# ACT reads the side banks behind the second exp of a burst; VectorE clips every fourth head of weights

## The reference

```python
x = L0_attn_x; xn = _layernorm(x, axis=-1)
return x + attn(xn) + ffn(xn)
# attn: scores = q k^T / sqrt(8); exp(clip(scores - max, -50, 50)) / (sum + 1e-6), times v, times Wout
# ffn:  q, k with rotary embedding; softmax attention, times Wo; x = rmsnorm(src + sa)
#       shared = swiglu(x W_shared_in) W_shared_out
#       h = swiglu(x W1_shared); routed = sum over 8 experts e of (h W2[e]) * w[:, e], two experts nonzero
#       out = rmsnorm(x + shared + routed)
```

## Time and profile before

| | before |
|---|---|
| median of 3 runs | 2111.24 us |
| the profiled execution's own time | 2110.22 us |
| its span, first to last instruction | 2108.4 us |
| TensorE busy | 1957.9 us (93%) |
| VectorE busy | 1629.0 us (77%) |
| ACT busy | 1442.8 us (68%) |
| GpSimd busy | 1135.9 us (54%) |
| granted TensorE clock, mean | 0.993 |

### The profile page before, as it was taken

One profiled execution on the slowest core, in us unless ns is written; L12 is line 12 of the kernel. 1 busy time (PEld: TensorE's weight loads), 2 busy tenths in 40 slices (PEclk: granted clock), 3 DMA queues, 4 the chain that ended last, 5 costly groups with the idle time before them and its releaser, 6 DMA issues.

```text
span 2108.4 us, 43905 instructions
## 1 busy us (share of the span) xinstructions
PE 1957.9 (93%) x10694; PEld 602.4 (29%) x10694; DVE 1629.0 (77%) x2948; ACT 1442.8 (68%) x2993; POOL 1135.9 (54%) x1695
## 2 busy tenths in 40 slices
PE   4998899999999999999999999999999999999885
PEld 1222223232332323233232323323232222323232
DVE  3878897878879787887978788797978879797421
ACT  0367677777777777777777777777777777777752
POOL 1352637456473746647374664737466473746434
PEclk9999999999999999999999999999999999999997
DMA  2101010101101010110101010010101001010000
GB/s 92 43 27 50 28 53 31 56 27 53 36 24 56 29 57 26 52 36 25 56 28 58 26 55 32 26 56 27 59 26 54 31 27 56 26 56 18 22 0 16
DMA packets 79167, 81.93 MB, mean 39 GB/s; under 512 B 14716, under 2 KB 66172, under 8 KB 78844
## 3 DMA queue, kind: packets, MB, share of 16 engines
q1 hardware_dynamic: 78984, 80.20, 11.2%
HBM read 11.36 MB, written 4.19 MB: 7 GB/s over the span
## 4 chain that ended last, share of the span: by engine, by line
PE 71%; DVE 12%; issue 7%; ACT 6%; POOL 2%; SPq 1%; DVEq 1%; ACTq 0%; DMA 0%; POOLq 0%
PE o_ps L501 19%; PE score_ps L467 19%; PE side_ps L580 10%; DVE negmax L757 7%; PE side_ps L567 6%; PE shift_ps L482 5%; PE side_ps L549 5%; PE side_ps L516 3%; ACT weights L614 3%; DVE x L785 2%; PE side_ps L553 2%; PE side_ps L538 2%; PE side_ps L572 1%; ACT spread L649 1%; DVE stats L846 1%
## 5 line engine op out<-in xcount | busy, mean ns | idle before, releaser
L757 DVE TENSOR_REDUCE negmax<-score_ps 128x1 f32<-128x512 f32 x2048 | 1308.4, 682 | 350.0 <-PE score_ps L467 326.4
L614 ACT ACTIVATE weights<-shift_ps 128x512 f32<-128x512 f32 x2048 | 1161.2, 599 | 517.9 <-PE shift_ps L482 491.1
L482 PE MATMUL shift_ps<-qt,kt 51*128 51x512 bf16 x2048 | 691.3, 387 | 46.7 <-ACT weights L614 42.3
L467 PE MATMUL score_ps<-kt,qt 48*128 48x512 bf16 x2048 | 658.1, 393 | 58.6 <-DVE negmax L757 32.3
L954 POOL TENSOR_SCALAR weights<-weights 128x2048 f32<-128x2048 f32 x256 | 485.1, 1895 | 138.5 <-ACT weights L614 109.8
L501 PE MATMUL o_ps<-weights,vt 128*32 128x512 f32 x4096 | 550.1, 610 | 0.3 <-POOL weights L954 0.3
L467 PEld LDWEIGHTS score_ps<-kt,qt 48*128 48x128 bf16 x2048 | 131.7, 94 | 683.7 <-DVE negmax L757 544.6
L580 PE MATMUL side_ps<-w_sb,hidden 128*128 128x512 f32 x512 | 252.2, 617 | 9.9 <-ACT spread L649 8.1
L482 PEld LDWEIGHTS shift_ps<-qt,kt 51*128 51x128 bf16 x2048 | 150.4, 93 | 220.7 <-ACT weights L614 210.5
L649 ACT ACTIVATE spread<-side_ps,gate 128x128 f32<-128x128 f32 x512 | 159.8, 377 | 26.3 <-PE side_ps L580 26.3
L567 PE MATMUL side_ps<-x1T,w_up_sb 128*128 128x512 f32 x256 | 148.2, 665 | 6.3 <-DVE hidden L817 4.7
(11 more groups left out here) (111 smaller groups left out, 1452.0 us busy)
## 6 DMA issues: line engine op xcount, KB each, us to landing
qt<-q_parts SPq DMA_DIRECT2D x768, 32.0 KB
kt<-k_parts SPq DMA_DIRECT2D x768, 32.0 KB
x_in<-in_x_dram SPq DMA_DIRECT2D x16, 256.0 KB, 2.7
xn_mid<-xn_new SPq DMA_DIRECT2D x16, 256.0 KB, 2.4
xn_old<-xn_mid SPq DMA_DIRECT2D x16, 256.0 KB, 2.4
res_new<-in_x_dram SPq DMA_DIRECT2D x16, 256.0 KB, 2.6
res_old<-res_new SPq DMA_DIRECT2D x16, 256.0 KB, 2.7
out_dram<-out_sb SPq DMA_DIRECT2D x16, 256.0 KB, 2.6
```

The source lines that it names most:

```text
L467: pe.matmul(score_ps[:, score_bank(a, t), :], qt[a][row:row + HROWS, slot, 128 * tile:128 * tile + 128], kt[a][row:row + HROWS, slot, :], ...
L482: pe.matmul(shift_ps[:, t % 2, :], kt[a][row:row + HROWS + MROWS, slot, 128 * tile:128 * tile + 128], qt[a][row:row + HROWS + MROWS, slot, ...
L614: act.activation(weights[:, i % 8, tile, :], shift_ps[:, t % 2, :], ACT.Exp, scale=SCALE).then_inc(weighed, 1)
L757: dve.tensor_reduce(negmax[:, i // 8, tile, i % 8:i % 8 + 1], score_ps[:, score_bank(a, t), :], AX.X, ALU.max, negate=True).then_inc(max_t ...
```

## The change

ACT's readers of side banks move by one to three steps: from the step after the job (an even step, whose exp is the first of its burst) to a later one. Most come to stand at odd steps; tanh moves from up + 1 to up + 3, and VectorE's product from up + 2 to up + 3; the expert scalings from job + 1 and + 2 to job + 2 and + 4; the high parts of q_plain and k_plain from + 1 to + 2, with VectorE's rests one step later. VectorE gets `clip` for heads 3, 7, 11 and 15, each in two halves of two tiles, with the floor alone; GpSimd keeps the other twelve, with floor and ceiling. The value groups of plain heads wait for both.

```diff
                     if a == PLAIN:
-                        pe.wait_ge(clip_pool, cnt(b, lag, H, 4 * quad + 4))
+                        pe.wait_ge(clip_pool, cnt(b, lag, 12, 3 * quad + 3))
+                        pe.wait_ge(clip_dve, cnt(b, lag, 8, 2 * quad + 2))
...
 (ACT, even half)
-                    if t == after("even", "max_rope1"):
+                    if t == after("even", "max_rope1", 2):
-                    part(b, 0, t, "q_rope", after("even", "qs_rope", 5), ROPE, roped[:, 0, :], q_parts, True)
+                    part(b, 0, t, "q_rope", after("even", "qs_rope", 4), ROPE, roped[:, 0, :], q_parts, True)
-                        if t == after("even", f"up{n}") and live(b, -2):
+                        if t == after("even", f"up{n}", 3) and live(b, -2):
-                    if t == 18:
+                    if t == 19:
-                    part(b, 0, t, "k_rope", after("even", "ks_rope", 11), ROPE, k_rest[:, :], k_parts, False)
-                    if t == after("even", "back_plain"):
+                    part(b, 0, t, "k_rope", after("even", "ks_rope", 10), ROPE, k_rest[:, :], k_parts, False)
+                    if t == after("even", "back_plain", 2):
-                    if t == after("even", "max_plain0"):
+                    if t == after("even", "max_plain0", 2):
-                    if t == 50:
+                    if t == 51:
-                        if t == after("even", f"v{n}", 1) and live(b, 0):
+                        if t == after("even", f"v{n}", 2) and live(b, 0):
...
 (ACT, odd half; max_plain1, back_rope, max_rope0 and the two copies of o_ps likewise one step on)
-                    part(b, 1, t, "q_plain", after("odd", "q_plain"), PLAIN, bank("q_plain"), q_parts, True)
-                    part(b, 1, t, "q_plain", after("odd", "q_plain", 3), PLAIN, q_rest[:, :], q_parts, False)
-                    part(b, 1, t, "k_plain", after("odd", "k_plain"), PLAIN, bank("k_plain"), k_parts, True)
+                    part(b, 1, t, "q_plain", after("odd", "q_plain", 2), PLAIN, bank("q_plain"), q_parts, True)
+                    part(b, 1, t, "q_plain", after("odd", "q_plain", 4), PLAIN, q_rest[:, :], q_parts, False)
+                    part(b, 1, t, "k_plain", after("odd", "k_plain", 2), PLAIN, bank("k_plain"), k_parts, True)
-                            if t == after("odd", f"exp{n}", 1 + half):
+                            if t == after("odd", f"exp{n}", 2 + 2 * half):
                                 weight_experts(b, n, half)
...
 (VectorE)
+            def clip(b, i, part):
+                if live(b, 0):
+                    dve.wait_ge(weighed, cnt(b, 0, 2 * UNIT, NT * i + 2 * part + 2))
+                    half = weights[:, i % 8, 2 * part:2 * part + 2]
+                    dve.tensor_scalar(half, half, FLOOR, None, ALU.max).then_inc(clip_dve, 1)
...
                     maximum(b, PLAIN, t)
+                    if t in (1, 2):
+                        clip(b + (-1), H - 1, t - 1)
...
-                        if t == after("even", f"up{n}", 2) and live(b, -2):
+                        if t == after("even", f"up{n}", 3) and live(b, -2):
...
                     maximum(b, ROPE, t)
-                    for job, rest, quarter in (("q_plain", q_rest, 9), ("k_plain", k_rest, 13)):
+                    if t > 16 and t % 16 in (1, 2):
+                        clip(b, t // 4 - 1, t % 16 - 1)
+                    for job, rest, quarter in (("q_plain", q_rest, 10), ("k_plain", k_rest, 14)):
...
 (GpSimd: the calls clip(b + (-1), 15), clip(b, 3), clip(b, 7) and clip(b, 11) are gone)
```

More of the change, by code:

```diff
@@ L273, in layer_kernel @@
         clip_pool = sem("clip_pool")
+        clip_dve = sem("clip_dve")
         valued = sem("valued")
@@ L711, in odd @@
                     weigh(b, 0, PLAIN, t)
-                    if t == after("odd", "max_plain1"):
+                    if t == after("odd", "max_plain1", 2):
                         copy_max(b, "max_plain1")
@@ L721, in odd @@
                         for half in range(2):
-                            if t == after("odd", f"exp{n}", 1 + half):
+                            if t == after("odd", f"exp{n}", 2 + 2 * half):
                                 weight_experts(b, n, half)
-                    if t == 18:
+                    if t == 19:
                         copy_o(b, "o_rope1", "o_rope0", 0)
-                    if t == after("odd", "back_rope"):
+                    if t == after("odd", "back_rope", 2):
                         copy_side(b, "back_rope", headsT[:, :])
-                    if t == after("odd", "max_rope0"):
+                    if t == after("odd", "max_rope0", 2):
                         copy_max(b, "max_rope0")
-                    if t == 50:
+                    if t == 51:
                         copy_o(b, "o_plain0", "o_rope1", 0)
@@ L1044, in even @@
             def even(b):
-                clip(b + (-1), 15)
                 if live(b, -3):
@@ L1080, in odd @@
                 third(b, 1, PLAIN, 1, k_rest, k_parts)
-                clip(b, 3)
                 clip(b, 4)
@@ L1087, in odd @@
                 mix(b, 2)
-                clip(b, 7)
                 if live(b, -1):
@@ L1101, in odd @@
                 mix(b, 5)
-                clip(b, 11)
                 mix(b, 6)
```

## The result

| | before | after |
|---|---|---|
| median | 2110.26 us (4 runs, 2108.23 to 2111.75) | 2277.01 us (4 runs, 2270.54 to 2290.05) |
| the profiled execution's own time | 2110.22 us | 2270.54 us |
| its span | 2108.4 us | 2268.8 us |
| granted TensorE clock, mean | 0.993 | 0.970 |

A forecast was written before the change was run, and what follows sets the result against it. TensorE's program order, busy 93%, was taken as the bound. Per round 10.95 us lost less 4.6 gained gave +6.3; 14 full rounds +88, ramps' clips some 2, on 2110.2: forecast 2201 us, 80% range 2150 to 2258.

The forecast's parts named there:

- six bank waits: TensorE waits at exp1, exp2, exp5 (1.6 us each), down0 (1.57), v0 (1.73) and k_plain (1.0), every round.
- part 2: Later readers release side banks later; lost per round: 4.8 us at expert jobs, 3.3 at down0 and v0, 1.0 at k_plain.
- the copies' gain: Ten places per round, late because a copy or scalings stood before a second exp, come on time: 3.5 us gained.
- the 0.95 us of the clips at steps 1 and 2: Even half's start: two VectorE half clips of 0.62 us, less 0.3 us of gaps, lose 0.95 us per round.
- the 0.9 us of VectorE's stretch: Around even steps 45 to 53, up2's later product and clips at 49/50 make VectorE late: 0.9 us lost per round.
- part 3: VectorE's clips: 8 more instructions per round at 0.70 us each; 0.95 and 0.9 us lost, 1.1 us gained per round.
- steps 17/18 ... slack enough: VectorE's clips at steps 17/18 lie ahead of exp0's 2.4 us job, so they cost nothing.
- clips fight GpSimd: Rival, 17%: VectorE's clips wait up to 1.9 us for GpSimd or cost 1.22 us; 3.0 us per round more, 2243 us.
- the gain of 1.1 us: Four scaled products at step 46, no longer beside a GpSimd clip, let bursts after steps 48 and 50 come on time.
- a round of 132 us: Sign that gains or clips were misjudged; the forecast itself had a round of 128 to 130 us.
- Late copies without a gain: Rival, 8%: ACT's backlog only moves one burst on, so the 3.5 us gain per round is missing: 2250 us.
- Stalls absorbed: Rival, 5%: VectorE and ACT catch up while TensorE stands, leaving 2.75 us gained per round: 2072 us.

The follow-up runs named there:

- experiment 3: The changed kernel, VectorE clips kept, with exp0, exp1, exp4, up0, up3 and q_plain read early again, all else late: 2099.96 us, ratio 0.9931 to before.
- kernel 2: The changed kernel with all sixteen clips on GpSimd again, moved readers kept: 2237.94 us, ratio 1.0592 to before.
- kernel 1: The kernel before with VectorE's clips of heads 3, 7, 11 and 15 alone, no copy moved: 2133.94 us, ratio 1.0094 to before.
- kernel 5: The kernel before with only the expert scalings late, at job + 2 and + 4: 2200.74 us, ratio 1.0419 to before.
- experiment 6: The changed kernel with exp0 alone released early, scaled by both pairs at job + 2: 2229.79 us, ratio 1.0547 to before.
- experiment 7: The kernel before with exp0's scalings alone late, at steps 20 and 22 instead of 19 and 20: 2144.36 us, ratio 1.0119 to before.
- experiment 8: The changed kernel with six banks released early, all clips on GpSimd, tanh of up1 to up3 at up + 2: 2084.79 us, ratio 0.9856 to before.
- kernel 9: As experiment 8, with the copies of xnT and x1T one step later: 2072.74 us, ratio 0.9801 to before.
- kernel 11: As kernel 9, with the clip of head 11 given to VectorE in halves at odd steps 49 and 50: 2044.78 us, ratio 0.9654 to before.
- kernel 10: As kernel 9, with GpSimd's clip of head 11 ahead of the mix of expert 5: 2059.6 us, ratio 0.9729 to before.

## Why the prediction was wrong in size

**Right: what decides.** That TensorE would stand at six bank waits, and how long, held to 0.1 us a piece in the burst distances (part 2); the copies' gain held (3.5 forecast, 3.7 measured, the shift's waits for ACT down from 408 to 205); so did the 0.95 us of the clips at steps 1 and 2, and the 0.9 us of VectorE's stretch. VectorE's half clip was put at 0.70 us from three rows of other operations, and undisturbed it takes 0.68. Undoing the six waits turned +8.0% into -0.7% (experiment 3), so the sign came out right for the stated reason.

**Wrong in part 3, "steps 17/18 ... slack enough".** I checked that VectorE had time there, not what GpSimd was doing. Head 3's second half meets clip 4 and takes 2.28 us: 1.41 x 14 = 20 us. The rival "clips fight GpSimd" had the mechanism and 17%, but priced it at steps 1/2, 33/34 and 49/50. Of those, 33/34 shows halves of 0.75 and 0.92 us without harm to TensorE, the others none in the loop. The sign that I had given for it, a mean over 0.9 us for the clip's row, is there, at 922 ns:

```profile
L767 DVE TENSOR_SCALAR weights<-weights 128x1024 f32<-128x1024 f32 x128 | 118.0, 922 | 0.0
```

**Wrong in part 3, the gain of 1.1 us.** "That clip is gone from GpSimd and clip 10 will be over": the clip in the earlier trace rows was clip 10. Instead of -1.1 came +0.55, 1.65 x 14 = 23 us. It could have been counted in the trace of before: the clips of a round stand in the order of the list. That it became a loss, and not nothing, depends on the phase: kernels 2 and 3 show neither here, kernel 1 +0.52, and kernel 5, without a clip on VectorE, +0.36. What sets it wasn't isolated.

**Left out: the clock.** The sum put it at nothing: no term and no rival had it, and the rows of before gave no hint, its clock being 0.993. For rounds 2 to 14, which have no edge effects, the account is: 140 us more than before; forecast 13 x 6.3 = 82; the steady terms came out at 8.9 a round (the table's 9.7 less the 0.8 that is the clock's) instead of 6.35, 13 x 2.55 = 33 more; 25 are left for 18 falls, 1.4 us each, near the 1.6 of the rounds with a fall behind exp2 and the 1.6 to 2.2 of experiments 5 to 7. Outside these rounds: -5 us in rounds 0 and 1, and +25 from round 15 on, where the forecast had 8. Of these 25, 7.5 lie in round 15, near the forecast's 6.3, and 17.9 behind the last score, where 2 were forecast and all is busy time at the lower clock (above). 140 - 5 + 25 = 160, the difference of the spans. So the clock has some 25 + 18 = 43 us of it, more than either of the two wrong terms. The sum was made against one profiled execution; the median of after lies 6.5 us over its profiled one, whose mean clock, 0.970, is the highest of the four (the others 0.960 to 0.965).

**The signs.** The prediction named a round of 132 us as the sign that gains or clips were misjudged; the round is 133.6, and it was so, with the clock beside it. TensorE's busy share is 86% where near 90 was forecast, and GpSimd is 98 us less busy where it was 120.

**The rivals.** Late copies without a gain: refuted by the ten places, 3.7 us shorter together. Stalls absorbed: refuted, each wait costs its whole length, and the six together 8.9 us a round.

## What to carry to other kernels

When a reader is moved later, ask first when its bank is written again, and let only the readers with a spare bank go late: nearly the same edit cost 5.9% or gained 1.4%, by six places out of some thirty (experiments 2 and 8). Before giving VectorE an SBUF-to-SBUF operation, list what GpSimd runs at that very microsecond, by name and index; a start 0.15 us behind GpSimd's made 2.28 us of 0.68. And where a sum adds pauses to TensorE, put a price on its clock too: in this kernel pauses of 1.5 us cost a quarter to a half more than they lasted (26.1 us for 20.5, 142 for 115, 91 for 62 in experiments 7, 3 and 5).

## What the runs showed of the hardware that I had not expected

- A single pause of TensorE of 1.5 us, in a kernel that keeps it over 90% busy, can be followed by 3.4 us at half its clock; 13 rounds had 3 such falls with one pause a round, 18 with six; kernels 1 and 3, without these pauses, had 3 and 4, behind VectorE's longer stretch at the even half's start. An extra pause of 1.76 us (kernel 9) was followed by 6.8 us and more.
- GpSimd, 55% busy over the span, bounds the end of a round once TensorE's other waits are gone; a clip taken from it, which I had put at nothing, was worth 28 us between kernels 9 and 11, 15 of them against the reordered list of kernel 10.
- A VectorE pass of 128x1024 fp32 with one SBUF source takes 0.68 us, and 2.28 (at most 2.34) beside a GpSimd clip of 1.90 that began first. It goes the other way too: in kernel 1 GpSimd's clip took 2.36 us, started 0.07 us after a half clip of VectorE:

```profile
1235.05 0.68 DVE L767 TENSOR_SCALAR weights<-weights 128x1024 f32<-128x1024 f32 x1
1235.12 2.36 POOL L967 TENSOR_SCALAR weights<-weights 128x2048 f32<-128x2048 f32 x1 [0.28 <-POOL out_sb L1032]
```

- Operations of 128x128 with two SBUF sources are held as well: the four scaled products take 1.13 us undisturbed, 1.48 beside the end of a clip, 2.17 and 2.18 beside a mix (kernels 9 and 11), and 3.0 to 3.8 beside a clip and a mix.
